# A gated-attention and mixture-of-experts kernel: the weights of the first expert projections split in three parts, q's weights loaded first, and the first group's gates computed before the maximum of v's weights on VectorE

## What is computed

```python
def xattn(batch, latent, Wk, Wq, Wv):          # batch = ctx, latent = layernorm(x)
    keys = einsum('bpe,fe->bpf', batch, Wk); queries = einsum('ble,fe->blf', latent, Wq)
    values = einsum('bpe,fe->bpf', batch, Wv)
    weights = softmax(einsum('ble,bpe->blp', queries, keys) / sqrt(128))
    return einsum('blp,bpe->ble', weights, values)

def moe_attention(hidden):                     # hidden = layernorm(x), E = 16 experts
    logits = normalised(x) @ normalised(sim_matrix) - sigmoid(gates)
    mask = logits > 0, or the best two where no expert is above 0
    w = softmax(relu(logits) over the mask)
    q, k, v = [einsum('ne,neh->nh', w, einsum('nc,ech->neh', x, p)) for p in (q_proj, k_proj, v_proj)]
    o = softmax(q k^T / sqrt(128)) v
    return einsum('enh,ehc->nc', einsum('ne,nh->enh', w, o), o_proj)

x = x + tanh(g_xattn) * xattn(ctx, layernorm(x))
x = x + tanh(g_ffn) * moe_attention(layernorm(x))
```

## Time and profile before

| | |
|---|---|
| median of three runs | 800.28 us (799.4 to 3181.3) |
| the profiled execution | 799.99 us, its span 798.1 us |
| mean granted TensorE clock | 0.987 |
| TensorE busy | 776.1 us, 97% of the span |
| VectorE, ScalarE, GpSimd busy | 607.2, 433.8, 483.0 us |

### The profile page before, as it was taken

The page is one execution under the profiler, slowest core; times in us unless marked ns, Lnnn a source line. Parts: engine busy times, 40 slices in busy tenths (PEclk is TensorE's granted clock), DMA queues, the critical chain, the costliest instruction groups (busy, mean ns, idle before and its releaser), DMA issues.

```text
span 798.1 us, 13995 instructions
## 1 busy us (share of the span) xinstructions
PE 776.1 (97%) x3999; PEld 418.1 (52%) x3999; DVE 607.2 (76%) x2037; ACT 433.8 (54%) x1129; POOL 483.0 (61%) x703
## 2 busy tenths in 40 slices
PE   7489999999999999999999999999999999999998
PEld 6445545555455555545555554555555455544444
DVE  2977787878787787778777787877878786775648
ACT  5554645556555655655565565456556555544445
POOL 3276657674746757474675747567574755765534
PEclk9789999999999999999999999999999999999999
DMA  6564476563655636365563636546364654543100
GB/s 192 136 216 159 162 219 174 169 209 94 209 161 164 189 106 204 97 210 167 151 191 106 202 109 209 166 150 186 101 207 116 208 160 139 163 135 116 53 14 28
DMA packets 97476, 122.57 MB, mean 154 GB/s; under 512 B 14611, under 2 KB 69111, under 8 KB 97399
## 3 DMA queue, kind: packets, MB, share of 16 engines
q1 hardware_dynamic: 96679, 121.59, 49.6%
q10 hardware_dynamic: 720, 0.08, 0.1%
HBM read 97.32 MB, written 24.31 MB: 152 GB/s over the span
## 4 chain that ended last, share of the span: by engine, by line
PE 88%; DVE 5%; DMA 2%; POOL 1%; ACT 1%; issue 1%; SPq 0%; DVEq 0%; ACTq 0%; POOLq 0%
PE acc_q L1380 20%; PE acc_k L1380 20%; PE acc_v L1380 20%; PE y L1409 9%; PE oT_p L1409 9%; PE m L1489 2%; PE m L1553 2%; DVE x_all L1175 1%; PE oT_p L1641 1%; PE m L1480 1%; PE m L1539 1%; DMA stage<-in_L_ffn_q_proj_dram 1%; PE m L1469 1%; POOL zq L658 1%; PE m L1529 1%
## 5 line engine op out<-in xcount | busy, mean ns | idle before, releaser
L658 POOL TENSOR_TENSOR zq<-zq_full,zq 128x512 f16<-128x512 f32 x256 | 297.8, 1170 | 222.4 <-ACT zq L743 222.2
L743 ACT ACTIVATE zq<-zq_full 128x512 f16<-128x512 f32 x256 | 160.1, 636 | 224.1 <-DVE zq_full L1145 224.0
L1175 DVE SCALAR_TENSOR_TENSOR x_all<-y,w_out,x_all 128x128 f32<-128x128 f32 x356 | 122.2, 343 | 96.1 <-issue 69.5
L1380 PE MATMUL acc_q<-zq,w_hi 128*128 128x512 f16 x510 | 193.3, 379 | 1.0 <-POOL zq L658 1.0
L1380 PE MATMUL acc_k<-zq,w_hi 128*128 128x512 f16 x510 | 193.2, 379 | 0.0
L1380 PE MATMUL acc_v<-zq,w_hi 128*128 128x512 f16 x510 | 193.2, 379 | 0.0
L1145 DVE TENSOR_TENSOR zq_full<-wq_bc,x2T_p 128x512 f32<-128x512 f32 x256 | 167.8, 668 | 2.5 <-DMA wq_bc<-w_rows 1.7
L1175 DVE SCALAR_TENSOR_TENSOR x_all<-oT_p,w_out,x_all 128x128 f32<-128x128 f32 x356 | 121.5, 341 | 0.0
L673 POOL TENSOR_TENSOR x_all<-stage,x_all 128x128 f32<-128x128 f32 x240 | 100.4, 456 | 19.8 <-DVE x_all L1175 13.3
L1380 PE MATMUL acc_q<-zq,w_lo 128*128 128x512 f16 x255 | 96.6, 379 | 0.0
L1380 PE MATMUL acc_v<-zq,w_lo 128*128 128x512 f16 x255 | 96.6, 379 | 0.0
(11 more groups left out here) (253 smaller groups left out, 1091.4 us busy)
## 6 DMA issues: line engine op xcount, KB each, us to landing
wq_bc<-w_rows SPq DMA_DIRECT2D x128, 512.0 KB, 4.5
blk_rows<-stage SPq DMA_DIRECT2D x26, 256.0 KB, 2.7
stage<-blk_rows SPq DMA_DIRECT2D x104, 64.0 KB, 2.0
blk_rows<-v_blk SPq DMA_DIRECT2D x15, 256.0 KB, 2.0
v_mix<-blk_rows SPq DMA_DIRECT2D x60, 64.0 KB, 2.9
blk_rows<-pc_blk SPq DMA_DIRECT2D x15, 256.0 KB, 4.1
pcT<-blk_rows SPq DMA_DIRECT2D x60, 64.0 KB, 2.0
out_dram<-x_all SPq DMA_DIRECT2D x15, 256.0 KB, 6.7
```

Of the source, the lines that this page charges most:

```text
L658: nc.gpsimd.tensor_tensor(zq[:, 1, e % Z_SLOTS, :], zq_full[:, e % F_SLOTS, :], zq[:, 0, e % Z_SLOTS, :], ALU.subtract).then_inc(zq_lo_poo ...
L743: nc.scalar.activation(zq[:, 0, e % Z_SLOTS, :], zq_full[:, e % F_SLOTS, :], ACT.Copy).then_inc(zq_hi_done, 1)
L1175: nc.vector.scalar_tensor_tensor(out=rows(x_all, g, b0 + b), in0=bank[:, tok(j)], scalar=w_out[:, g % 2, e, b0 + b:b0 + b + 1], in1=rows(x ...
L1380: last = nc.tensor.matmul(acc[m][:], w[:, m, s, :], zq[:, half, s % Z_SLOTS, :], start=(s == 0 and n == 0), stop=(s == E - 1 and n == 2))
```

## The change

Only the head, body(0) and one place of body(1) change. Nothing is computed otherwise.

- SP loads Q's weights ahead of the contexts, and x for group 1 ahead of V's weights. The first gate spread is cut into its two experts, with a semaphore each.
- The split of Q, K and V goes in three parts, experts 0 to 3, 4 to 7 and 8 to 15 (`PARTS`), of which only the first stands ahead of the first zq product.
- TensorE makes px_transpose(0) and att_product(0) ahead of the other contexts, the scores of group 1 ahead of the gathered maximum, and its keep_busy products are spread differently (15 in place of 8 behind the contexts).
- VectorE makes the statistics of group 1 and all of group 0's gates ahead of the maximum of V's weights.
- ScalarE's x2_norm(0) comes ahead of kxT_out(3); x2_norm(1) comes ahead of zq_high of expert 4.
- GpSimd's first_rstd(2) moves from the head behind zq_low of expert 6, body(0) step 2.
- In body(1) the copy oT_high(0) comes ahead of zq_high of that step.
- O's split is one step later.

```diff
+PARTS = ((0, 4), (4, 8), (8, 16))
-        HIGH_AT = (0, 9)
-        LOW_AT = (0, 11)
+        HIGH_AT = (0, 10)
+        LOW_AT = (0, 12)
...
                 sp.wait_ge(kq_in, 16 * 2)
+                load_weights(Q, q_proj)
                 sp.dma_start(zq_full[0:S, 0:PRE].rearrange("p k (b c) -> p (k b) c", b=G),
                              c_v[:, G:G * (PRE + 1), :]).then_inc(ctx_pre_in, 16)
-                load_weights(Q, q_proj)
                 load_weights(K, k_proj)
+                load_x(1)
                 load_weights(V, v_proj)
-                load_x(1)
                 load_weights(O, o_proj)
                 load_x(2)
                 weight_rows(0)
-                for j in range(W_SLOTS):
+                for e, done in enumerate((wq_first_in, wq_in[0])):
+                    src = w_rows[0:1, G * e:G * (e + 1), :].rearrange("a r n -> (a r n)")
+                    sp.dma_start(wq_bc[:, 0, e], src.partition_broadcast(P)).then_inc(done, 16)
+                for j in range(1, W_SLOTS):
                     spread_q(0, j)
@@ GpSimd, head @@
                 zq_low(0, LEAD - 1)
-                first_rstd(2)
@@ GpSimd, body @@
                     for g, e in zq_at(i, s):
                         zq_low(g, e)
+                    if i == 0 and s == 2:
+                        first_rstd(2)
@@ ScalarE, head @@
-                ctxT_out(1)
                 pxT_out(0)
-                ctxT_out(2)
-                ctxT_out(3)
-                kxT_out(1)
-                vx_out(1)
-                for g in range(2, PRE + 1):
+                for g in range(1, PRE + 1):
+                    ctxT_out(g)
+                for g in range(1, PRE):
                     kxT_out(g)
                     vx_out(g)
                 x2_norm(0)
+                kxT_out(PRE)
                 x2T_out(0)
-                weight_high(Q)
                 x_norm(1)
+                vx_out(PRE)
                 gate_exps(0)
                 xnT_out(1)
                 x2T_move(0)
+                x_exps(1)
+                weight_high(Q)
                 weight_high(K)
-                x_exps(1)
                 pxT_out(1)
                 weight_high(V)
-                for e in range(LEAD):
+                weight_high(Q, 1)
+                weight_high(K, 1)
+                zq_high(0, 0)
+                weight_high(V, 1)
+                for e in range(1, LEAD):
                     zq_high(0, e)
+                x2_norm(1)
@@ ScalarE, body @@
+                    if i == 1 and s == Y_FIRST:
+                        oT_high(0)
                     for g, e in zq_at(i, s):
                         zq_high(g, e)
+                    if i == 0 and s == 1:
+                        weight_high(Q, 2)
+                        weight_high(K, 2)
+                    if i == 0 and s == 2:
+                        weight_high(V, 2)
@@ VectorE, head @@
                 weight_max(K)
+                first_stats(1)
                 setup_gate()
-                weight_max(V)
-                share_largest(0)
-                first_stats(1)
-                weight_scales(0)
                 x2_norm_inverse(0)
                 gate_logits(0)
                 gate_mask(0)
                 gate_softmax(0)
+                weight_max(V)
+                x_max(1)
+                share_largest(0)
+                weight_scales(0)
                 weight_low(Q)
-                x_max(1)
                 weight_low(K)
                 x_sum(1)
                 zq_scale(0, 0)
+                weight_low(V)
                 zq_scale(0, 1)
-                weight_low(V)
                 zq_scale(0, 2)
                 x1_add(1)
                 second_stats(1)
                 zq_scale(0, 3)
-                first_stats(2)
+                weight_low(Q, 1)
+                weight_low(K, 1)
@@ VectorE, body @@
+                    if i == 0 and s == 0:
+                        weight_low(V, 1)
+                    if i == 0 and s == 1:
+                        first_stats(2)
+                    if i == 0 and s in (2, 3, 4):
+                        weight_low((Q, K, V)[s - 2], 2)
@@ TensorE, head @@
                 vx_product(0)
+                px_transpose(0)
+                att_product(0)
                 for g in range(1, PRE + 1):
                     ctx_transpose(g)
-                px_transpose(0)
-                kx_product(1)
-                att_product(0)
-                vx_product(1)
-                for g in range(2, PRE + 1):
+                for g in range(1, PRE + 1):
                     kx_product(g)
                     vx_product(g)
                 pe.wait_ge(kxT_sb, 3)
-                keep_busy(8)
+                keep_busy(1)
                 x2_transpose(0)
-                pe.wait_ge(vx_sb, PRE + 1)
-                gather_max(0, acc[V])
+                keep_busy(1)
...
+                keep_busy(3)
+                gather_max(0, acc[V])
+                pe.wait_ge(vx_sb, PRE + 1)
+                spread_max(0, acc[K])
+                keep_busy(1)
                 px_transpose(1)
+                keep_busy(2)
                 att_product(1)
+                keep_busy(3)
```

More of the change, by code:

```diff
@@ L411, in vx_bank, with split_part @@
             return (acc[V], oT_p, acc[K])[g - 1] if 1 <= g <= PRE else m0
+        def split_part(t, m, part):
+            experts = slice(*PARTS[part]) if m < O else slice(0, E)
+            return t[:, m, experts].rearrange("p e h -> p (e h)")
         def ctx_slot(g):
@@ L877, in pxT_out, with oT_high @@
                                          px_mix[:].rearrange("p i b n -> p b i n"), ACT.Copy).then_inc(pxT_sb, 1)
+            def oT_high(g):
+                wait(act, oT_ps, g + 1)
+                wait(act, y_ps, PAIRS_Y * (g - 1))
+                nc.scalar.activation(oT[:, g % 2, 0, :], oT_p[:], ACT.Copy).then_inc(oT_hi_done, 1)
             def head():
@@ L971, in body @@
                         kxT_out(g1)
-                    if s == Y_FIRST and has(gc):
-                        wait(act, oT_ps, gc + 1)
-                        wait(act, y_ps, PAIRS_Y * (gc - 1))
-                        nc.scalar.activation(oT[:, gc % 2, 0, :], oT_p[:], ACT.Copy).then_inc(oT_hi_done, 1)
+                    if s == Y_FIRST and i > 1 and has(gc):
+                        oT_high(gc)
                     if s == 10 - sooner(i) and has(g1):
@@ L1064, in weight_scales, with weight_low @@
                     nc.vector.tensor_scalar(out_scale[:], out_scale[:], tanh_f[:], None, ALU.mult).then_inc(scales_done, 1)
-            def weight_low(m):
-                dve.wait_ge(hi_done[m], 1)
+            def weight_low(m, part=0):
+                dve.wait_ge(hi_done[m], part + 1)
                 nc.vector.scalar_tensor_tensor(
-                    out=w_lo[:, m].rearrange("p e h -> p (e h)"), in0=stage[:, m].rearrange("p e h -> p (e h)"),
-                    scalar=w_up[:, m:m + 1], in1=w_hi[:, m].rearrange("p e h -> p (e h)"),
-                    op0=ALU.mult, op1=ALU.subtract).then_inc(lo_done[m], 1)
+                    out=split_part(w_lo, m, part), in0=split_part(stage, m, part), scalar=w_up[:, m:m + 1],
+                    in1=split_part(w_hi, m, part), op0=ALU.mult, op1=ALU.subtract).then_inc(lo_done[m], 1)
             def blocks_transposed(dst, src, done):
@@ L1376, in experts @@
                 for m in (Q, K, V):
+                    for part, (first, _) in enumerate(PARTS):
+                        if (i, s) == (0, first):
+                            pe.wait_ge(hi_done[m], part + 1)
+                            pe.wait_ge(lo_done[m], part + 1)
                     if s == 0:
```

15 lines of the change are left out of this document (10 added, 5 removed).

## The result

The changed kernel took 806.54 us (median of five runs, 804.6 to 807.28) against 800.28 for the kernel before (one of its five runs took 3181.3 us, for a reason that is not known, and is left out of the ratio); the ratio is 1.0069, 95% interval 1.0058 to 1.0081. Four runs more in a second comparison gave 804.63 (804.46 to 805.08) against 800.39, 1.0052 (1.0035 to 1.0068). So it is 4 to 6 us slower: within 2%, but more than the comparison's own uncertainty. The forecast was 801.1, with 796.8 to 803.8 as its range: the direction and the chain were right, the size was not. It is the fastest of the five; the other four were not profiled.

The account below looks back on a forecast made before the run. TensorE, busy 97%, was taken as the bound, behind a head set by other engines until about 57 us. 799.99 + 0.9 (logits) + 1.3 (clock) - 1.1 (output projection) = 801.1 us, range 796.8 to 803.8.

Parts of the forecast that it names:

- The head: Start to first expert: gates at 26.2 instead of 29.62, scale 6 us later, expert 0 at about 40.2 against 43.21.
- The lock: Body(0): GpSimd stands still under VectorE's w_lo; six pieces, three of 0.6 and three of 1.15, 5.2 us together.
- The logits: Group 1's logits in expert 5: x2T behind x_norm(2) and GpSimd's chain starts them at 57.8 against 56.92, 0.9 later.
- The clock: TensorE behind group 1's logits: half clock after standing still costs 1.3 us, between 0 and 1.7.
- The output projection: Body(1): with oT_high(0) ahead of the high half the wait of 1.03 goes; 1.1 us saved, between 0 and 1.2.
- The sum: Whole kernel: 799.99 + 0.9 + 1.3 - 1.1 = 801.1 us.
- Part of the lead survives: Body(0): pieces miss GpSimd, clock holds, logits start at 55.4; 797.4 us, down to 796.2; chance 0.27.
- The slower rival: Head: contexts land late or half clock ahead of px, logits at 59.3; 803.0 us; chance 0.23.
- sign of 27.5: Head: if the gates start later than 27.5, the slower case (803.0 us, chance 0.23) holds.
- the second rival: Body(0): part of the lead is kept to group 1's logits; 797.4 us, down to 796.2; chance 0.27.
- The likeliest case: Body(0): the lead is used up before group 1's logits; 801.1 us, own range 799.6 to 802.6; chance 0.45.

Follow-up runs that it names:

- the run with fillers: Eighteen 128x128 products that nobody reads put on TensorE ahead of expert 5's first matmul, against the changed kernel: 803.96 us.
- the second profile: The changed kernel run again without any edit, as the base of the comparisons on its chip: 804.63 us.
- x2T first: ScalarE's x2T_out(1) put right behind expert 6's high half, ahead of the copy (V,2), against the changed kernel: 800.37 us, 0.9994 of the kernel before.

## Why the prediction was wrong

The mechanism was right, and two terms of the sum failed by their size. The first is the step from expert 0 to group 1's logits: they were put at 57.8 and came at 59.99, of which 0.9 us is the later head and 1.4 the chain over GpSimd, where the exclusion with the w_lo pieces was priced too low. The second is the clock: 1.3 us in the sum and 1.7 at the most, where the runs show 1.7 to 3.0 and this profile 2.97. The range also left little room for a head that varies by 3.8 us between executions (first expert 40.87 to 44.64 in eight profiles with the same head). Held against its own steps:

- **The head.** Q's maximum started at 13.88, a whole us ahead of the forecast of 14.9, and it gave nothing: VectorE then waited for the attention product. The gates' first logit came at 26.55 (26.2), w_blk was done at 31.08 (30.7), the scale at 35.83 (35.3), the first low half at 40.11 (39.3), the first expert at 40.87 (40.2). From the gates on every step was right and a little late; 0.8 us at the low half. The gate rows, put at 37, were there when VectorE needed them at 38.03.
- **The lock.** From the end of one low half to the end of the chain behind it, second_rstd(1) was reckoned at 2.55 us and took 2.8, second_norm(1) at 2.25 and took 2.6, first_rstd(2) at 2.35 and took 3.2 (54.54 to 57.77): its two small instructions waited for one piece almost in full and for the end of another. This last term was mis-sized by 0.9. Part of it is the pieces themselves: taken at 0.6 and 1.15 us, a quarter and a half of a whole w_lo, they took 0.7 and 1.27. The row of rnorm that the prediction reads beside the rule of two inputs (57.23) has one input only, so it shows an instruction held up but is no case of that rule as the prediction puts it.
- **The logits.** 0.9 of a later start, 0.2 + 0.3 + 0.9 of these chains and -0.1 elsewhere make 59.99 in place of 57.8. The wait for the maximum came out as sized (2.23, forecast 2.4), but the piece ahead of it waited for ScalarE's copy and not, as forecast, for GpSimd. The wait for x2T was sized too short (5.10, forecast 4). The bound of 59.5 was passed, because it counted the pieces and not the late start.
- **The clock.** Measured: 2.97 by the row of 55.70:65.94, and 2.9 by the run with fillers. This step failed in its argument: it took the 2.56 us that the kernel before needed to come back to 2.4 GHz as a constant. Here it took 5.95 us from the first matmul, and 4.12 in the second profile. The 3.4 us at half rate behind the bound of 1.7 stand in no row of the prediction; the kernel before has another stretch at half clock in its head that has this length (PE busy for all of it, clock 0.50), but it is not a return behind a standstill:

```profile
11.61:15.03 3.42, 3.42 (x21) 3.42 (x21) 0.48 (x1) 2.94 (x11) 0.00 (x0) 0.50 0.96 275
```

- **The output projection.** -1.1, right: the wait of 1.03 is gone, and it is 1.2 when the part is undone.
- **The sum.** 2.2 us at the logits and 1.4 behind them (2.97 less 1.3, with 0.3 of small gains) are the 3.5 us between 801.1 and the profiled 804.6. The further 1.9 up to the first median would fit the head's variation from run to run, since the later first experts of the related kernels (up to 44.6) give as much, but this is not shown: none of the four slower runs was profiled.
- **The rivals.** "Part of the lead survives" needed the pieces to miss GpSimd and the clock to hold; neither did. The slower rival named two conditions, contexts that land late and half clock ahead of px. Both were then seen in related kernels' profiles (17.8 us; half clock from 11 or 17), so its 0.23 was too little. Its 803.0 is the nearest of the forecasts, but not for its reason: in the profile of the result the clock is at half from 11.3 to 14.7, as in the kernel before, and x2_norm(0) still starts at 22.27 (22.0 was forecast) and the gates at 26.55, below its sign of 27.5. That 796.2 is the lower end of the second rival is a slip; a whole us less than 797.4 is 796.4. The likeliest case and this rival should have been added, not set side by side.

## What to carry to other kernels

A lead at one place is worth what is left of it where the bounding engine next waits: follow it to that place, and look first at what stands ahead of the instruction that releases it. Here x2T_out stood behind a copy and a norm it did not need; moving it one step gave 4.3 us, as much as the whole change had cost. A wait that is inside a longer one has no price, and removing it only lengthens the other.

Where two engines exclude each other, count for a chain of tiny instructions the rest of the long instruction that runs beside them, not their own length. And when a change makes TensorE stand still for microseconds, take the clock's loss as half of a stretch that may last several microseconds beyond the restart (3.4 to 6.0 here). Fillers in the gap removed it in the one profile taken; the median of that kernel did not show the gain.

## What the chip showed that was not expected

- A GpSimd instruction on 128x4 took 1.21 or 1.09 us instead of 0.23 beside a VectorE w_lo of two SBUF inputs, and 0.23 again when the piece was moved away; a w_lo took 1.84 instead of 1.27 under a low half. The Trainium skill, page SBUF — State Buffer, section Who interferes with whom, has this as its exclusive lock, and the traces agree in both directions.
- At the first expert the return to full clock took 2.56 us of dense matmuls in the kernel before and 0.6 with x2T first. Behind the same wait of 5.10 us it took between 3.9 and 6.0 us in six profiles.
- Half clock between 17 and 25 us lengthens the head by 1.3 to 3 us, in some profiles and not in others.
- The contexts' 462 KB, issued between 8.15 and 8.34, released TensorE between 16.8 and 17.8 in the five profiles where it waited for them.
